# Two transformer layers on one core: layer 1's first norms inside layer 0's FFN, roots on VectorE, a reordered opening, and four rope remainders on VectorE

## The reference

```python
h = layernorm(x) * (1 + ca) + sa;  x = x + ga * attention(h)
h = layernorm(x) * (1 + cb) + sb;  x = x + gb * ffn(h)
```

## Time and profile before

| | |
|---|---|
| median of 3 runs | 777.65 us (776.88 to 778.69) |
| the profiled execution | 778.5 us, its span 776.7 us |
| instructions | 12379 |
| granted TensorE clock, mean over the span | 0.992 |

### The profile page before, as it was taken

The page is one execution under the profiler, slowest core; times in us unless marked ns, Lnnn a source line. Parts: engine busy times, 40 slices in busy tenths (PEclk is TensorE's granted clock), DMA queues, the critical chain, the costliest instruction groups (busy, mean ns, idle before and its releaser), DMA issues. The chain is left out here.

```text
span 776.7 us, 12379 instructions
## 1 busy us (share of the span) xinstructions
PE 721.5 (93%) x4376; PEld 620.7 (80%) x4376; DVE 556.8 (72%) x1263; ACT 447.5 (58%) x924; POOL 372.5 (48%) x403
## 2 busy tenths in 40 slices
PE   6979989999999999999999799999979999789997
PEld 4858878888888888888888689997768778577787
DVE  4656786678766787767776788776579788566666
ACT  2756656667566676666655343322578776546432
POOL 2685556635766357653451330002756545205773
PEclk8999999999999999999999999999999999999999
DMA  7000000000000000004000040004100000000001
GB/s 250 14 8 8 8 22 15 14 2 14 22 15 8 8 15 14 14 8 170 7 8 8 9 128 1 1 1 126 39 0 2 1 1 1 0 4 0 1 1 55
DMA packets 19115, 19.85 MB, mean 26 GB/s; under 512 B 2158, under 2 KB 17006, under 8 KB 19054
## 3 DMA queue, kind: packets, MB, share of 16 engines
q1 hardware_dynamic: 17934, 18.40, 7.3%
q10 hardware_dynamic: 1120, 0.66, 0.3%
HBM read 18.01 MB, written 1.05 MB: 25 GB/s over the span
## 5 line engine op out<-in xcount | busy, mean ns | idle before, releaser
L633 ACT ACTIVATE at_probs<-at_probs,at_negmax 128x128 f32<-128x128 f32 (+7 forms) x128 | 99.6, 778 | 31.8 <-DVE at_negmax L736 29.7
L935 POOL TENSOR_TENSOR at_swapped<-at_swapped,at_sin 128x512 f32<-128x512 f32 x40 | 52.1, 1302 | 136.0 <-ACT at_swapped L611 136.0
L736 DVE CUSTOM_DVE_ANT_0 at_probs<-at_scores,causal 128x128 f32<-128x128 f32 (+7 forms) x128 | 96.1, 751 | 16.8 <-PE at_scores L59 16.2
L524 PE MATMUL at_turn<-ident_sb,at_probs 128*128 128x128 f32 x576 | 85.0, 274 | 13.2 <-DVE at_full_T_lo L752 11.1
L524 PEld LDWEIGHTS at_turn<-ident_sb,at_probs 128*128 128x128 f32 x576 | 66.5, 140 | 21.8 <-issue 8.4
L626 ACT ACTIVATE at_edge_T_hi<-at_turn 128x128 fp32r<-128x128 f32 (+3 forms) x128 | 55.5, 434 | 33.2 <-PE at_turn L524 32.8
L57 PE MATMUL at_scores<-at_kT_hi,room 128*128 128x512 f32 (+1 forms) x192 | 66.4, 346 | 3.4 <-DVE at_negmax L736 3.4
L626 ACT ACTIVATE at_full_T_hi<-at_turn 128x512 fp32r<-128x512 f32 x64 | 38.3, 598 | 49.5 <-PE at_turn L524 47.4
L58 PE MATMUL at_scores<-at_kT_lo,room 128*128 128x512 f32 (+1 forms) x192 | 66.7, 347 | 0.0
L59 PE MATMUL at_scores<-at_kT_hi,room 128*128 128x512 f32 (+1 forms) x192 | 66.3, 345 | 0.0
L752 DVE TENSOR_TENSOR at_edge_T_lo<-at_turn,at_edge_T_hi 128x128 fp32r<-128x128 f32 (+3 forms) x128 | 61.3, 479 | 1.1 <-ACT at_edge_T_hi L626 0.8
(11 more groups left out here) (405 smaller groups left out, 2292.3 us busy)
## 6 DMA issues: line engine op xcount, KB each, us to landing
at_wq_in<-L_attn_Wqkv SPq DMA_DIRECT2D x16, 128.0 KB, 2.2
at_wo_in<-L_attn_Wo SPq DMA_DIRECT2D x16, 128.0 KB, 2.0
staging<-L_ffn_routed_w SPq DMA_DIRECT2D x7, 256.0 KB, 4.8
ff_wmod<-L_wmod SPq DMA_DIRECT2D x1, 1536.0 KB, 6.2
at_wmod<-L_wmod SPq DMA_DIRECT2D x1, 1024.0 KB, 8.6
staging<-L_ffn_w_gate SPq DMA_DIRECT2D x1, 1024.0 KB, 5.2
staging<-L_ffn_w_up SPq DMA_DIRECT2D x1, 1024.0 KB, 7.3
staging<-L_ffn_w_down SPq DMA_DIRECT2D x1, 1024.0 KB, 9.7
```

The costliest lines, as they stand in the source:

```text
L524: mm = pe.transpose(p_turn[t % 2][:, b - b0, :], probs[:, s % 4, b * P:(b + 1) * P], m.ident[:, :])
L633: act.activation(row, row, ACT.Exp, scale=-1.0, bias=negmax[:, unit % 4:unit % 4 + 1], accum_out=rowsum[:, unit // NT % 2, i:i + 1])\
L736: dve.tensor_tensor_reduce(out=probs[:, s % 4, 0:width], in0=p_scores[s % 2][:, 0:width], in1=m.causal[:, S - width:], scale=-1.0, scalar= ...
L935: turning = pool.tensor_tensor(swapped[:, r % 2, :], swapped[:, r % 2, :], sin[:, cols], ALU.mult)
```

## The change

It touches five places.

1. **Roots.** `variance_roots` and ACT's square roots of variances are gone. DVE makes the inverse root by itself: a shift of the float's bits as an integer, then three Newton steps, 11 small instructions (eps, start, 3 x 3) each waiting for the last. ACT's table loads for them go or move.
2. **Opening of attention 0.** x is loaded as two transfers of four tiles, one by SP and one by ACT; ACT issues identity and mask ahead of its first activation; of PE's five warm matmuls two come behind the modulation columns; DVE takes the statistics of tiles 4 to 7 as one group, makes their roots behind the first half's remainders, and the first cosine product ahead of the value weight's remainder.
3. **Ropes.** For the first four roped tensors POOL ends with the high part, and DVE makes the remainder (`rope_lo`).
4. **FFN 0.** Layer 1's modulation weights for rows come during attention 0 (two more transfers by SP); their products with c (`mod_rows`) stand at the block's start, its warm matmuls shrink from 16 to 2. In the loop, for tiles 0 to 3: roots by pairs (`row_roots`), norms on ACT (`normalize`), modulation on POOL, squares and root on ACT (with a table load there and back), inverse on DVE, scaling on POOL, transposes on PE in unit 7, split on ACT and POOL. POOL also bounds the gates and splits all of layer 1's attention weights, ACT rounds the projection weights. Behind the loop DVE makes h of tiles 4 and 5.
5. **Attention 1.** The first block is gone. The remaining one starts with four projections of the first half (`early_jobs`); beside them tiles 6 and 7 are added, normed and all of 4 to 7 scaled and turned; then come the second half's first projections. `k10` moves from the loop to the early jobs. The experts' weights are loaded in this block. POOL starts with the first normalization. The sigmoid's table is loaded at the block's end, not in FFN 1.

```diff
+def inverse_roots(dve, m, chain, tiles):
+
+
     cols = slice(tiles[0], tiles[-1] + 1)
-    dve.wait_ge(m.sqrt_out, n)
-    chain.run(dve.reciprocal(rstd, root))
-    chain.run(dve.tensor_tensor(rough, rstd, rstd, ALU.mult))
-    chain.run(dve.tensor_tensor(rough, rough, vareps, ALU.mult))
-    chain.run(dve.tensor_scalar(rough, rough, -0.5, 1.5, ALU.mult, ALU.add))
-    chain.run(dve.tensor_tensor(rstd, rstd, rough, ALU.mult))
+    rough, rstd, vareps, var = m.tiny[:, 1, cols], m.rstd[:, cols], m.vareps[:, cols], m.meanvar[:, cols, 1]
+    as_int = mybir.dt.int32
+    chain.run(dve.tensor_scalar(vareps, var, EPS, None, ALU.add))
+    chain.run(dve.tensor_scalar(rstd.bitcast(as_int), vareps.bitcast(as_int), -0.5, float(0x5F3759DF), ALU.mult, ALU.add))
+    for _ in range(3):
+        chain.run(dve.scalar_tensor_tensor(out=rough, in0=rstd, scalar=-0.5, in1=vareps, op0=ALU.mult, op1=ALU.mult))
+        chain.run(dve.tensor_tensor(rough, rough, rstd, ALU.mult))
+        chain.run(dve.scalar_tensor_tensor(out=rstd, in0=rough, scalar=1.5, in1=rstd, op0=ALU.add, op1=ALU.mult))
...
-                keep_warm(pe, early_banks[1], m.causal, 5)
+                keep_warm(pe, early_banks[1], m.causal, 3)
                 pe.wait_ge(wmod_in[0], 16)
                 pe.wait_ge(c_silu, 1)
                 mod_columns(0)
+                keep_warm(pe, early_banks[1], m.causal, 2)
                 pe.wait_ge(const_in, 32)
...
                 act.dma_start(craw[:, 0, :], a["L0_c"]).then_inc(c_in, 16)
-                for half in range(2):
-                    act.dma_start(m.x[:, 4 * half + 2:4 * half + 4, :], x_rows[:, 4 * half + 2:4 * half + 4, :]).then_inc(x_in[half], 16)
                 act.dma_start(craw[:, 1, :], a["L1_c"]).then_inc(c_in, 16)
+                act.dma_start(m.x[:, 4:NT, :], x_rows[:, 4:NT, :]).then_inc(x_in[1], 16)
+                act.dma_start(m.ident[:, :], a["ident"]).then_inc(const_in, 16)
+                act.dma_start(m.causal[:, S - P:], a["mask"]).then_inc(const_in, 16)
                 act.wait_ge(c_in, 32)
                 act.activation(m.csil[:, :, :], craw[:, :, :], ACT.Silu).then_inc(c_silu, 1)
-                act.dma_start(m.ident[:, :], a["ident"]).then_inc(const_in, 16)
-                act.dma_start(m.causal[:, S - P:], a["mask"]).then_inc(const_in, 16)
-                variance_roots(act, m, FIRST_TILES, 1)
+                act.wait_ge(zeros_done, 1)
+                act.activation(m.tables[:, 0:1], m.causal[:, 0:1], ACT.Exp)
                 act.wait_ge(wk_loaded, 16)
...
+                    if unit < 2:
+                        rope_lo(2 + unit)
...
+                def rope_lo(r):
+
+                    out, c = FIRST_ROPES[r]
+                    cols = slice(c * BANK, (c + 1) * BANK)
+                    dve.wait_ge(rope_hi, r + 1)
+                    dve.tensor_tensor(out.lo[:, cols], plain[:, r % 2, :], as_f32(out.hi[:, cols]), ALU.subtract).then_inc(rope_done, 1)
...
-                    chain.run(pool.tensor_scalar(out.hi[:, cols], turned, 1.0, 1.0, ALU.mult, ALU.mult))
+                    high = pool.tensor_scalar(out.hi[:, cols], turned, 1.0, 1.0, ALU.mult, ALU.mult)
+                    if r < len(FIRST_ROPES):
+                        high.then_inc(rope_hi, 1)
+                        return
+                    chain.run(high)
+                    if r == len(FIRST_ROPES):
+                        pool.wait_ge(rope_done, r)
...
+                pe.wait_ge(m.mod_in, 32)
+                mod_rows(0)
                 turn_x(0)
                 turn_x(1)
-                keep_warm(pe, idle_bank, m.room, 9)
+                mod_rows(1)
+                keep_warm(pe, p_gate[:, 0:2, :].rearrange("p e t -> p (e t)"), m.room, 2)
                 for u in range(UNITS):
                     c, half = divmod(u, 2)
                     if not half:
                         pe.wait_ge(hx_ready, c + 1)
                     wide(u, wg, p_gate, silu_done, gate_mm)
-                    if 2 <= u < UNITS - 1:
+                    if u >= 2:
                         down(u - 2)
+                    if u == 7:
+                        turn_g()
...
+                    if u == 0:
+                        read_rows()
+                    if u == 1:
+                        attention_weights_hi()
                     if u in (2, 4):
                         scale_shift(u // 2 + 1)
+                    if u == 4:
+                        normalize(0)
+                    if u == 5:
+                        mean_squares(0)
+                    if u == 6:
+                        normalize(1)
+                        mean_squares(1)
+                        roots()
+                        load_table(act, m, ACT.Silu, 0)
+                    if u == 7:
+                        turned_hi()
                     magnitude(u)
...
+                def row_roots(c):
+                    tiles = (2 * c, 2 * c + 1)
+                    stats(c)
+                    variances(dve, m, chain, tiles)
+                    inverse_roots(dve, m, chain, tiles)
+                    spread(dve, m, tiles).then_inc(rstd_done, 1)
...
+                inverse_roots(dve, m, chain, LAST_TILES)
                 low_x(1)
-                inverse_roots(dve, m, chain, LAST_TILES, 4)
                 norm(LAST_TILES)
                 for u in range(UNITS):
                     c, half = divmod(u, 2)
                     multiply(u)
-                    if u >= 3 and half and u < UNITS - 1:
+                    if u in (3, 5):
                         add(c - 1)
-                    if u == UNITS - 1:
-                        add(CHUNKS - 2)
+                    if u == 5:
+                        row_roots(1)
+                    if u == 6:
+                        inverses()
+                    if u == 7:
+                        stats(2)
+                        variances(dve, m, chain, (4, 5))
                     sparsify(u)
-                    if u >= 3 and half and u < UNITS - 1:
-                        stats(c - 1)
-                stats(CHUNKS - 2)
-                add(CHUNKS - 1)
-                stats(CHUNKS - 1)
+                    if u == 1:
+                        small_weights()
+                    if u == 3:
+                        row_roots(0)
+                    if u == 6:
+                        add(2)
+                inverse_roots(dve, m, chain, (4, 5))
...
+                pool.wait_ge(mod_read, 3)
+                bounded_gate(0)
+                pool.wait_ge(w_hi, 2)
+                pool.tensor_tensor(late.wq.lo, late.wq_in, as_f32(late.wq.hi), ALU.subtract)
+                pool.tensor_tensor(late.wv.lo, late.wv_in, as_f32(late.wv.hi), ALU.subtract)
+                low_x(2)
+                pool.wait_ge(w_hi, 4)
+                pool.wait_ge(up_mm, 3)
...
+                pool.wait_ge(up_mm, 4)
+                pool.wait_ge(m.staged1, 80)
+                for n in range(H1):
+                    chain.step(pool.tensor_tensor(late.wo_in[:, n, :], late.wo_in[:, n, :], m.gate[:, 1, 0, :], ALU.mult))
+                low_x(3)
+                chain.settle()
+                chain.run(pool.tensor_scalar(late.wo.hi, late.wo_in, 1.0, 1.0, ALU.mult, ALU.mult))
+                mod_rows(0)
+                pool.wait_ge(up_mm, 6)
+                chain.step(pool.tensor_tensor(late.wo.lo, late.wo_in, as_f32(late.wo.hi), ALU.subtract))
+                mod_rows(1)
+                pool.wait_ge(late.inverted, 1)
+                for n in FIRST_TILES:
+                    pool.tensor_scalar(g_row[:, n, :], late.h_row[:, n, :], late.inv[:, n:n + 1], 1.0, ALU.mult, ALU.mult).then_inc(g_done, 1)
+                for k in range(KD):
+                    pool.wait_ge(g_hi, k + 1)
+                    pool.tensor_tensor(m.hT.lo[:, k, 0:BANK], g32[:, k, :], as_f32(m.hT.hi[:, k, 0:BANK]), ALU.subtract)
+                bounded_gate(1)
...
+        early_jobs = [("k", 0, 0), ("qq", 0, 0), ("v", 0, 0), ("k", 1, 0)]
+        jobs = early_jobs + [("k", 0, 1), ("qq", 0, 1)]
+        first = [p_scores[1][:, 0:BANK], p_scores[1][:, BANK:S]]
+        first += [p_turn[n][:, :, :].rearrange("p a b -> p (a b)") for n in range(2)] + [p_proj[:, :], p_att[:, :]]
+        jobs += [("v", 0, 1), ("k", 1, 1), ("q", 2, 0), ("q", 2, 1), ("q", 3, 0), ("q", 3, 1)]
...
+                for n, job in enumerate(early_jobs):
+                    project(n, *job)
+                turn_g()
+                for n, job in jobs_of(-1)[len(early_jobs):]:
...
+                job_high(0, *jobs[0])
+                mean_squares((4, 5))
+                job_high(1, *jobs[1])
+                mean_squares((6, 7))
+                roots()
+                job_high(2, *jobs[2])
+                normed_rows()
+                job_high(3, *jobs[3])
+                turned_hi()
...
+                chain = m.chain.on(dve)
+                for n in (6, 7):
```

(26 more changed lines are left out.)

480 lines of the change are left out of this document (224 added, 256 removed).

## The result

The changed kernel took 782.76 us in the median of 5 runs (781.49 to 784.14), the one before 777.65; the ratio is 1.0064, with a 95% interval of 1.0047 to 1.0082. It is slower by 5 us, where a gain of 4.7 us was forecast, and lies above the range. The profiled execution took 782.76 us, with a span of 780.7 against 776.7 before.

What follows compares the result with a forecast made beforehand. PE looked busy for 93%, but partly with keep-warm matmuls before attention 1; in the FFN, DVE set the pace. Terms -4.6 + 14.5 - 14.0 - 3.0 + 2.4 = -4.7 gave a 773.0 us median, own range 769 to 776.

Steps and rivals of the forecast that it cites:

- The term of 14.5: FFN 0 as a whole: 14.5 us more, ending at 546.8 against 532.3, with DVE losing time beside POOL.
- the bound of 529.3: FFN 0: without any loss to POOL, DVE's sum would end at 529.3; PE then sets about +1.5.
- up to 2 us of the range: PE's clock may fall in its 7 us wait before FFN 0's second up pass; up to 2 us of range.
- Attention 0: -4.6 forecast: Attention 0's opening and ropes together: 4.6 us less, bounds 1 and 7.
- The ropes' part: Attention 0's ropes: four remainders of 1.29 leave POOL (5.2 us) and cost DVE 0.69 each in idle time.
- the opening's 3 us: Attention 0's opening: PE's first transposes at about 12.2, 3.0 us earlier; bounds 0 to 4.5.
- both waits go: Attention 0's opening: PE's 4.1 us wait for identity and mask and DVE's 2.17 for ACT's root both vanish.
- Attention 0 gives nothing back: Rival, chance 0.10: in attention 0 PE's value products take what POOL wins; -1 in place of -4.6, total 776.6.
- Attention 1's opening: -14.0 forecast: Attention 1's opening: first score 14.3 us behind the block's start in place of 28.3; -14.0, bounds -12.5 and -15.5.
- Its loop: -3.0 forecast: Attention 1's loop: a 1.25 us wait for POOL and one key projection go; -3.0, bounds -1 and -4.
- Tail: +2.4 forecast: Tail: two roots on the path, 11 steps for 5, 1.2 us more each; +2.4.
- The slower rival: Rival, chance 0.18: in FFN 0's masks DVE pays POOL's whole time, losing 20.2 for 12.4; +7.8, total 780.8.

Runs made afterwards that it cites:

- experiment 2: The changed kernel with 9 and 4 idle matmuls filling PE's wait in attention 1's opening: 780.1 us, 1.0035 of the kernel before.
- experiment 3: The changed kernel with 4 and 6 idle matmuls filling PE's waits in attention 0's opening: 781.33 us, 1.0042 of the kernel before.
- experiment 4: The changed kernel with PE's waits filled by idle matmuls in both attentions' openings and FFN 0 (16 and 11 there): 777.48 us, 1.0001 of the kernel before.
- experiment 11: The kernel of experiment 4 with DVE taking attention 1's first maximum ahead of the second query remainder: 777.94 us, 1.0014 of the kernel before.
- experiment 5: The kernel before with only attention 0 taken from the changed kernel: 777.44 us, 0.9997 of the kernel before.

## Why the prediction was wrong, point by point

- **Where the gain and the price lie: right.** The first score comes 11.7 us sooner behind the block's start, and the masks pay in FFN 0. The term of 14.5 was met (14.6) by luck, by errors that cancel: the part before the first product was sized 2.9 too high (one DVE instruction per POOL instruction also for steps that wait on each other), the loop 2.2 too low (a 1024-column instruction cost 2.2 at once) and the part behind it 0.8 too low. Two other traces of the same FFN code (experiments 2 and 3) have 13.2 or 13.3 in its place. A slip besides: the bound of 529.3 takes the first gate's 2.3 us off twice; nothing hangs on it.
- **The clock: the step that failed.** The prediction gave the clock "up to 2 us of the range" and no term, with the reason that DVE sets the pace where PE waits. But PE comes out of several waits at half clock, and the matmuls behind lie on the path: 0.43 us apart in place of 0.23. Filling the waits gave back 4.9 us (1.0064 to 1.0001), of which about 1.1 is a collision that moved (experiment 4). The clock's part is at most some 3.8 of the miss of 9.8 (782.76 against 773.0), and not half of it.
- **Attention 0: -4.6 forecast, 0 measured** (0.9997 alone), perhaps 1.3 with full clock. Two steps failed. The ropes' part took POOL's chain for the bound and DVE's 0.69 as free: the remainder took 1.77 beside POOL, or stood 2.3 in DVE's queue; undone, it cost nothing that shows. And the opening's 3 us became 1.8 by the first score; "both waits go" held for DVE's wait for the root, while the wait for the mask mostly became shorter, until 12.6 to 12.9. "Attention 0 gives nothing back", at 0.10, was the right rival.
- **Attention 1's opening: -14.0 forecast, -11.7 in the profile.** The steps were right to 0.1 us up to the transposes; most of the rest is the clock (14.5 behind the start with the wait filled, for 14.3).
- **Its loop: -3.0 forecast, -0.3 in the profile.** Removing two waits (1.25 for POOL, the key's job in slot 3) was priced at what they showed. The fifth maximum stands as far behind the first score as before (12.6 us for 12.75). What holds it now is argued, not shown: by my reading another chain, the second query remainder and the value projection of slot 1 (experiment 11).
- **Tail: +2.4 forecast, +2.6 in the profile.** The steps were right. The wait of PE that the longer root makes at the end of attention 1 was given no clock term; where the clock falls behind it, the tail is 1.6 longer.
- **The slower rival** had the right sign. The Trainium skill (SBUF — State Buffer, section on who interferes with whom) says that a DVE instruction with two SBUF inputs contends with a GpSimd instruction that reads SBUF, and that the loser waits for the whole of it; the row of 2.62 beside 2.42 agrees. As a rule for the sum the rival gave 780.8, 2 us short, and its price for the port was too high: 20.2 us, where the same instructions lost about 16.3 (15.4 from the first product on, 0.9 beside the first gate's steps). The FFN took what was forecast; the kernel is slower for the other reasons above.

In all, for the profiled execution: 3.4 (attention 0), 0.1 (FFN 0), 2.3 (opening), 2.7 (loop), 0.2 (tail): 8.7 us, from -4.7 to +4.0.

## What to carry to other kernels

A wait of PE that "costs nothing" is paid behind it if its clock falls: before moving work so that PE waits in new places, price the matmuls behind each wait at half clock, or fill it with matmuls on a free bank. After filling, look at what else moved: idle matmuls also delay whoever waits for PE, and part of a gain may be that. Work given to an idle POOL beside a DVE that sets the pace is not free, and moving one piece may bring the next one forward onto DVE. And where two waits are removed from a chain, look for the third that ends almost as late before adding them up.

## What the runs showed of the hardware

- The half stretches fall in other places from one execution to the next: for the same opening of attention 0 at 8.7 and 22.4 (changed kernel), 9.5 (experiment 2), 12.8 and 23.0 (experiment 5). The first scores came at 32.6, 30.7 and 33.4 us. The clock alone doesn't make that difference: the transposes began at 11.3, 10.8 and 12.8, the last when the mask had landed. In experiment 3 twelve executions took 778.2 to 782.5. One profile doesn't price a step in such a stretch to better than 2 us.
- Half clock off the path can help: in units 2 and 3 of the FFN it kept POOL's products away from DVE's masks, 19.9 to 20.2 us in place of 21.2 (experiment 4).
- A DVE instruction of 0.42 us took 2.62 beside one POOL instruction of 2.42, and PSUM products stayed at 1.21 to 1.22 beside POOL in all units.
